# Norm sums taken four chunks at a time inside stage one, with two weight steps and a row centring moved to other places

## The chip, the cores and the metric

The kernel runs on one core of one Trainium2 chip. The metric is the device time of one execution in microseconds, the median of several runs. A core has five engines with a queue of instructions each: PE (TensorE, matrix products and transposes), DVE (VectorE), ACT (ScalarE), POOL (GpSimd) and SP (SyncE, which here only issues DMAs). Semaphores order the queues against each other; within a queue instructions start in order. A wait at the head of a queue holds all that stands behind it.

## The reference

Inputs are x and ctx, each 128 x 64 x 128 in fp32. Two layers are computed, each added to x:

```
q  = layernorm(x)                                 # no gain, no bias
pq = prob(q); pk = prob(ctx)                      # t = tanh(.)*0.499+0.5;  p = t / (sum(t) + 1e-8)
sid = (pq - pk) @ (log pq - log pk).T             # per batch, 64 x 64
att = softmax(-sid / sqrt(128)) @ ctx
f   = (ctx - att) @ W_diff.T + b_diff + q
h   = layernorm(f) * ln_g + ln_b
o   = gelu(h @ W1.T + b1) @ W2.T + b2 + f         # hidden size 512
x   = x + layernorm(o) * ln_g + ln_b
x   = x + (fp16(fp8(layernorm(x))) @ fp16(fp8(Wf)).T + bf)
```

What matters here is `prob`. With s the sum of tanh over the 128 features of a row, its norm is 0.499 s + 64. The kernel never divides: it forms pq - pk from tanh with a gain and a shift for each row, and takes log pq - log pk as the difference of two logarithms plus the logarithm of the ratio of the two norms. So for each row it needs the reciprocals of two norms, two gains, a shift and the ratio.

## The kernel before, in words

**Tiles.** The 8192 rows are 64 tiles of 128 rows (two batches each); four tiles are a chunk, so there are 16 chunks (`NC`). TQK holds the tanh of all of q and ctx, F holds q and later f and the output, X holds x plus the bias row, PV the values. The orders below are written out by hand: `run_steps` calls a function once per step, and `at(lag)` is the chunk that is `lag` steps behind. Nothing else plans the work.

**Stage one** (`phase1` on each engine) runs over the chunks. ACT takes the tanh of a ctx chunk (L507) with the sum of each row, copies two products out of PSUM (L512, L518), and takes the tanh of the q chunk two steps behind (L523). DVE takes the statistics of the x chunk (L754, then six small instructions, L711 to L726), adds the product of W_diff and its bias to F for the chunk three steps behind (L759), and makes q of the chunk one step behind (L780). POOL takes the power -0.5 of the variance (L362) and adds the bias row b to X (L368). PE transposes ctx (L951) and multiplies with W_diff (L960, L969). SP loads ctx and x; the load of x for a chunk waits for the variance of the chunk two before (L308), since the small buffers alternate, and each queue of loads is in order.

Into some steps the preparation of the weights is laid: W1 and W2 are transposed on PE at step lag 2 of chunk 6 (`W_AT`, L971), copied by DVE (L762, L764), and split in an upper and a lower part, W1h by ACT (L529), W1l by DVE in the last step before q of chunk 15 (L768). PE computes W1 times ln_b (`b1_ps`, L984) after all of stage one, and DVE adds b1 to it (L787).

**The norms** are taken by DVE in `take_norms` (L728): one instruction for 0.499 s + 64 (L735), the reciprocal (L738), then HALFK, GAINK, GAINQ, NRATIO and SHIFT (L740 to L745), small instructions over one number per row and tile. It is called for chunks 0 to 13 (`NORMS`) when chunk 13 has reached L759, and for the last two after stage one. Between its steps DVE waits for its own previous instruction.

**Stage two** runs over 17 pieces (`pairs`): 15 of four tiles and two of two. For a piece, ACT and POOL form the gain and shift of ctx in `diff_c` (L559, L380; ACT the first half of the tiles), DVE adds the part of q for three tiles (L810) and POOL for the fourth (L388, L391). ACT takes the logarithms of both sides (L569); DVE and POOL form the difference (L818; L396, L399) with LRATIO, the logarithm of NRATIO (L573). PE transposes both (L1056, L1062), ACT copies them out (L594, L596), PE forms the scores (L1044), ACT takes the exponential (L579), PE the attention product (L1029), DVE normalises it and adds it to F (L832, L838). The lags are 0, 1 and 2. Before it, DVE centres the row b2 (L678 to L682), and ACT loads another table (L533). DVE's `dve.wait_ge(pq_ready, NC)`, PE's `pe.wait_ge(pq_ready, NC)`, and POOL's and ACT's waits for `norms` stand ahead of their first pieces.

**Stage three** (`phase3`) runs over 17 pieces: the MLP, the second normalisation, the fp8 layer and the stores. The change touches nothing in it.

## Time and profile before

| | us |
|---|---|
| median of 3 runs (261.57, 262.82, 263.22) | 262.82 |
| the profiled execution | 262.99 |
| its span, as the profile has it | 261.1 |

| stage | from, to |
|---|---|
| one (tanh, products) | 0 to about 62.8 |
| change of stage | 61.5 to 66.5 |
| two (attention) | 66.5 to 128.5 |
| three | the rest |

Busy shares of the span: PE 80%, DVE 86%, ACT 83%, POOL 72%. A busy share is an average over stages; the start times of instructions show who waits. Durations of neighbouring instructions on an engine overlap a little: the start of the next one, not the end of this one, tells how fast an engine goes. TensorE runs at one of two levels of clock, and a granted clock of 0.50 is the lower one.

### The profile page before, as it was taken

Reading aid. Unit: us, or ns where it says so; the run is one execution under the profiler, and the core shown is the slowest. Engines: PE = TensorE matmul, PEld = TensorE weight load, DVE = VectorE, ACT = ScalarE, POOL = GpSimd, SP = SyncE. Lnnn points to the kernel's source line nnn. Section 1 sums busy time; section 2 is a strip of 40 time slices with the busy share of each in tenths; the row PEclk is TensorE's granted clock in tenths of the full one; section 3 lists DMA queues with packets and bytes.
Section 4 is the critical chain, followed back from the end, with each engine's and each line's share of the span. In section 5 each row is a group of like instructions: output and inputs, shape, how many; then the busy total and the mean of one; then the engine's idle time right before and its main releaser. Section 6 shows DMA issues by size and latency. Waiting matters only on the chain.

```text
span 261.1 us, 5925 instructions
## 1 busy us (share of the span) xinstructions
PE 209.4 (80%) x1723; PEld 176.3 (68%) x1723; DVE 225.0 (86%) x843; ACT 216.2 (83%) x774; POOL 188.9 (72%) x250
## 2 busy tenths in 40 slices
PE   2676676754499888887899999999999999996711
PEld 1664554533387666666689988888889888895600
DVE  2899999988879999999525889999999999999892
ACT  4599999998889999989997888988898887776521
POOL 2477666764899999991885796969697888666552
PEclk9999999795569999999999999999999999999765
DMA  5667554540000000000328189897978888977922
GB/s 140 188 201 204 158 154 135 154 113 1 1 0 3 0 3 3 1 3 4 40 32 91 12 100 135 122 133 110 151 115 132 129 125 128 137 121 121 103 61 61
DMA packets 51360, 23.65 MB, mean 91 GB/s; under 512 B 9856, under 2 KB 51200, under 8 KB 51328
## 3 DMA queue, kind: packets, MB, share of 16 engines
q0 software_dynamic: 15856, 7.87, 28.0%
q1 hardware_dynamic: 35040, 15.21, 21.9%
q10 hardware_dynamic: 432, 0.20, 0.4%
q8 instruction: 14, 0.23, 0.4%
q14 instruction: 18, 0.15, 0.2%
HBM read 9.37 MB, written 4.19 MB: 52 GB/s over the span
## 4 chain that ended last, share of the span: by engine, by line
POOL 28%; DVE 23%; ACT 20%; issue 13%; PE 11%; DMA 3%; SPq 0%; POOLq 0%; DVEq 0%; ACTq 0%
POOL F L407 7%; POOL xrstd L448 7%; ACT TQK L523 6%; ACT TQK L507 6%; POOL orstd L442 6%; DVE q_c L810 5%; POOL F L454 5%; DVE LN_c L818 5%; DVE F L838 5%; PE bank L1011 3%; ACT PV L518 3%; DMA LN_c<-in_ctx_dram 3%; ACT vT_c L512 2%; PE bank L960 1%; DVE F L863 1%
## 5 line engine op out<-in xcount | busy, mean ns | idle before, releaser
L1011 PE MATMUL bank<-W2T,TQK 128*128 128x128 f32 x512 | 68.7, 282 | 2.6 <-ACT TQK L545 2.5
L1011 PEld LDWEIGHTS bank<-W2T,TQK 128*128 128x128 f32 x512 | 64.0, 194 | 8.5 <-ACT TQK L545 4.0
L545 ACT ACTIVATE TQK<-bank,b1c 128x512 f32<-128x512 f32 (+1 forms) x68 | 44.5, 661 | 10.7 <-PE bank L1004 10.4
L448 POOL TENSOR_TENSOR xrstd<-xvar,pow_c 128x4 f32<-128x4 f32 (+1 forms) x17 | 18.5, 1090 | 23.2 <-DVE xvar L726 23.2
L362 POOL TENSOR_TENSOR xrstd<-xvar,pow_c 128x4 f32<-128x4 f32 x16 | 16.8, 1051 | 21.5 <-DVE xvar L726 21.5
L1002 PE MATMUL bank<-hTh,W1h 128*128 128x512 f32 (+1 forms) x68 | 30.4, 447 | 0.8 <-DVE hTl L801 0.8
L407 POOL DMA_DIRECT2D F<-rows x17 | 26.0, 1529 | 5.6 <-DVE E_c L796 5.6
L1003 PE MATMUL bank<-hTl,W1h 128*128 128x512 f32 (+1 forms) x68 | 26.1, 384 | 0.0
L1004 PE MATMUL bank<-hTh,W1l 128*128 128x512 f32 (+1 forms) x68 | 25.9, 382 | 0.0
L960 PE MATMUL bank<-WdT,vT_c 128*128 128x128 f32 x128 | 20.5, 309 | 4.8 <-ACT vT_c L512 4.6
L951 PE MATMUL bank<-ident,LN_c 128*128 128x128 f32 x64 | 12.3, 322 | 13.9 <-DMA LN_c<-in_ctx_dram 13.9
L960 PEld LDWEIGHTS bank<-WdT,vT_c 128*128 128x128 f32 x128 | 17.8, 215 | 7.5 <-ACT vT_c L512 7.4
L883 DVE TENSOR_SCALAR LN_c<-F,xmv,xrstd 128x128 fp8e4<-128x128 f32 x64 | 17.9, 343 | 4.8 <-POOL xrstd L448 4.6
L368 POOL TENSOR_TENSOR X<-X,rows 128x512 f32<-128x512 f32 x16 | 20.3, 1271 | 2.0 <-DVE F L780 2.0
L507 ACT ACTIVATE TQK<-LN_c 128x128 f32<-128x128 f32 x64 | 19.3, 329 | 2.3 <-DMA LN_c<-in_ctx_dram 2.3
L454 POOL DMA_DIRECT2D F<-rows x14 | 18.6, 1326 | 2.9 <-issue 2.9
L951 PEld LDWEIGHTS bank<-ident,LN_c 128*128 128x128 f32 x64 | 8.3, 162 | 18.2 <-DMA LN_c<-in_ctx_dram 18.0
L523 ACT ACTIVATE TQK<-F 128x128 f32<-128x128 f32 x64 | 19.5, 340 | 0.8 <-DVE F L780 0.8
L1029 PE MATMUL bank<-PV,E_c 64*64 64x129 f32 x256 | 18.7, 286 | 1.6 <-ACT E_c L579 1.6
L810 DVE SCALAR_TENSOR_TENSOR q_c<-TQK,GAINQ,q_c 128x128 f32<-128x128 f32 x49 | 17.8, 413 | 2.0 <-POOL q_c L380 2.0
L630 ACT ACTIVATE TQK<-F 128x128 f32<-128x128 f32 x64 | 19.0, 313 | 0.2 <-DVE F L858 0.2
L863 DVE SCALAR_TENSOR_TENSOR F<-F,orstd,rows 128x128 f32<-128x128 f32 x64 | 19.1, 359 | 0.0
(129 smaller groups left out, 645.2 us busy)
## 6 DMA issues: line engine op xcount, KB each, us to landing
F<-rows POOLq DMA_DIRECT2D x29, 256.0 KB, 4.7
LN_c<-in_ctx_dram SPq DMA_DIRECT2D x16, 256.0 KB, 3.0
X<-in_x_dram SPq DMA_DIRECT2D x16, 256.0 KB, 3.3
out_dram<-F SPq DMA_DIRECT2D x15, 256.0 KB, 2.3
LN_c<-in_L_xattn_W_dram SPq DMA_DIRECT2D x1, 256.0 KB, 3.5
lT_c<-in_L_xattn_W_dram SPq DMA_DIRECT2D x1, 256.0 KB, 3.7
F<-rows POOLq DMA_DIRECT2D x2, 128.0 KB, 4.8
out_dram<-F SPq DMA_DIRECT2D x2, 128.0 KB, 1.8
```

The lines of the kernel that those rows point to most:

```text
L407: pool.dma_start(tiles(chunk(F, k)), over_tiles(b2_r, k.g), accum_op=ALU.add).then_inc(b2_added[k.n % 3], 16)
L448: pool.tensor_tensor(buf(xrstd, x1, G), buf(xvar, x1, G), pow_c[:, 0:x1.g], ALU.pow).then_inc(x1_rstd, 1)
L454: pool.dma_start(tiles(chunk(F, x1)), over_tiles(bf_r, x1.g), accum_op=ALU.add).then_inc(bf_added[x1.n % 3], 16)
L507: last = act.activation(all_tile(TK, k, i), tile(ctx_c, k, i), ACT.Tanh, accum_out=per_tile(SUMK, k, i))
L523: last = act.activation(all_tile(TQ, k, i), all_tile(F, k, i), ACT.Tanh, accum_out=per_tile(SUMQ, k, i))
L545: act.activation(hid(m, j), m1_bank(m, j), ACT.Gelu, bias=b1c[:, j:j + 1]).then_inc(gelu_ready, 1)
L810: last = dve.scalar_tensor_tensor(out=tile(diff_c, k, i), in0=all_tile(TQ, k, i), scalar=per_tile(GAINQ, k, i), in1=tile(diff_c, k, i), op ...
L960: last = pe.matmul(P_B[k.n % 3][:, i * D:(i + 1) * D], tile(vT_c, k, i), WdT[:, :], start=(i == 0), stop=False, skip_group_check=True)
L1002: pe.matmul(ps, w_hi, buf(hTh, m), start=True, stop=False)
L1003: pe.matmul(ps, w_hi, buf(hTl, m), start=False, stop=False)
L1004: pe.matmul(ps, w_lo, buf(hTh, m), start=False, stop=True).then_inc(m1_ps, 1)
L1011: last = pe.matmul(M2_B[m.buf][:, i * D:(i + 1) * D], hid(m, j)[:, i * D:(i + 1) * D], W2T[:, j * D:(j + 1) * D], start=(j == 0 and i == 0 ...
```

## The change

1. `take_norms` is cut in three: `norm_sums`, `norm_inverses`, `norm_gains`. They are called for four chunks at a time (`NORM_CUTS`), the first three groups inside stage one, when chunks 4, 8 and 12 reach L759, with the statistics laid between sum and reciprocal and q between reciprocal and gains. The last group is taken in stage two behind piece 1.
2. W1l moves from the last step to the step in which chunk 10 reaches L759; the products for b1 on PE and DVE's addition of b1 move to the steps of chunks 10 and 11.
3. The centring of the b2 row moves from ahead of stage two to behind piece 2.
4. POOL forms all four tiles of `diff_c` for piece 0, those of piece 1 right behind its part of piece 0, and adds the bias row to X of chunk 15 only behind piece 15 of stage two. ACT has no tile of piece 0. POOL's scratch tile is another.
5. LRATIO is taken in two calls: chunks 0 to 11 ahead of the first logarithms, the rest behind those of piece 10.
6. Waits: each engine waits for the group of norms that a piece needs (`wait_norms`) when the piece begins a group. PE enters stage two when 14 chunks, not 16, have reached L759, and waits for the rest and for b1 ahead of the first attention product.

```diff
@@ -89,7 +89,8 @@
     EARLY = 2
-    NORMS = NC - 2
+    NORM_CUTS = (0, 4, 8, 12, NC)
+    LRATIOS = NORM_CUTS[-2]
@@ -174,7 +175,7 @@
         r16_c = LN_c[:, 2 * C:3 * C].bitcast(F16)
-        qpart_c = RNORM[:, :]
+        qpart_c = E_c[:, C:C + D]
@@ -196,7 +197,11 @@
         def by_act(k):
-            return k.g // 2
+            return k.g // 2 if k.n > 0 else 0
+        def wait_norms(eng, k):
+            if k.live and k.n in NORM_CUTS[:-1]:
+                eng.wait_ge(norms, NORM_CUTS.index(k.n) + 1)
@@ -271,7 +276,8 @@
         vT_ps, vT_sb, P_ps, P_sb = sem("vT_ps"), sem("vT_sb"), sem("P_ps"), sem("P_sb")
-        norm_step, halfk_ready, norms, lratio = sem("norm_step"), sem("halfk_ready"), sem("norms"), sem("lratio")
+        norm_sum, norm_inv, halfk_ready, norms, lratio = (
+            sem("norm_sum"), sem("norm_inv"), sem("halfk_ready"), sem("norms"), sem("lratio"))
@@ -354,6 +360,11 @@
             pool.memset(PV[:, :].rearrange("p (t w) -> p t w", w=D + 1)[:, :, D:D + 1], -1.0).then_inc(consts, 1)
+            def add_to_x(k):
+                pool.wait_ge(q_ready, k.n + 1)
+                pool.tensor_tensor(tiles(chunk(X, k)), tiles(chunk(X, k)), over_tiles(b_r, k.g),
+                                   ALU.add).then_inc(xb_ready, 1)
@@ -361,45 +372,50 @@
                 k = at(1)
-                if k.live:
-                    pool.wait_ge(q_ready, k.n + 1)
+                if k.live and k.n < NC - 1:
...
                         pool.wait_ge(br_in, 16)
-                    pool.tensor_tensor(tiles(chunk(X, k)), tiles(chunk(X, k)), over_tiles(b_r, k.g),
-                                       ALU.add).then_inc(xb_ready, 1)
+                    add_to_x(k)
             run_steps(chunks, 1, phase1)
+            def kparts(k):
+                wait(pool, dT_ps, k.n - 1)
+                wait_norms(pool, k)
+                for i in range(by_act(k), k.g):
+                    last = pool.tensor_scalar(tile(diff_c, k, i), all_tile(TK, k, i), per_tile(GAINK, k, i),
+                                              per_tile(SHIFT, k, i), ALU.mult, ALU.add)
+                last.then_inc(kpart, 1)
...
                 if k.live:
-                    wait(pool, dT_ps, k.n - 1)
-                    if is_piece(k, NORMS):
-                        pool.wait_ge(norms, 2)
-                    for i in range(by_act(k), k.g):
-                        last = pool.tensor_scalar(tile(diff_c, k, i), all_tile(TK, k, i), per_tile(GAINK, k, i),
-                                                  per_tile(SHIFT, k, i), ALU.mult, ALU.add)
-                    last.then_inc(kpart, 1)
+                    if k.n > 1:
+                        kparts(k)
...
                         pool.wait_ge(kpart, k.n + 1)
-                        if is_piece(k, 0):
-                            pool.wait_ge(norms, 2)
...
                                            ALU.add).then_inc(diff_pool, 1)
+                        if is_piece(k, 0):
+                            kparts(pairs[1])
...
                             pool.wait_ge(lratio, 1)
+                        if is_piece(k, LRATIOS):
+                            pool.wait_ge(lratio, 2)
...
                                            ALU.subtract).then_inc(lr_pool, 1)
-            pool.wait_ge(norms, 1)
+                if is_piece(k, NA - 2):
+                    add_to_x(chunks[NC - 1])
+            kparts(pairs[0])
@@ -553,8 +569,7 @@
                 wait(act, dT_ps, k.n - 1)
-                if is_piece(k, NORMS):
-                    act.wait_ge(norms, 2)
+                wait_norms(act, k)
@@ -568,9 +583,9 @@
                                    scale=TANH_GAIN).then_inc(ln_ready, 1)
-                if is_piece(k, 0):
-                    act.wait_ge(norms, 2)
-                    act.activation(LRATIO[:, :], NRATIO[:, :], ACT.Ln).then_inc(lratio, 1)
+                if is_piece(k, LRATIOS - 2):
+                    act.wait_ge(norms, len(NORM_CUTS) - 1)
+                    act.activation(LRATIO[:, LRATIOS * G:], NRATIO[:, LRATIOS * G:], ACT.Ln).then_inc(lratio, 1)
@@ -613,8 +628,8 @@
             act.wait_ge(sel_ready, 1)
-            act.wait_ge(norms, 1)
-            kparts(pairs[0])
+            act.wait_ge(norms, len(NORM_CUTS) - 2)
+            act.activation(LRATIO[:, 0:LRATIOS * G], NRATIO[:, 0:LRATIOS * G], ACT.Ln).then_inc(lratio, 1)
@@ -725,18 +740,25 @@
                 dve.tensor_tensor(buf(xvar, k, G), buf(xgap, k, G), mv[:, :, 1], ALU.add).then_inc(done, 1)
-            def take_norms(first, end, part):
-                cols, n = slice(first * G, end * G), 2 * part
-                sums, norm, rnorm = (t[:, :].rearrange("p (s t) -> p s t", s=2)[:, :, cols] for t in (SUM, NORM, RNORM))
-                dve.wait_ge(tanh_k, end)
-                dve.wait_ge(tanh_q, end)
+            def of_norms(part):
+                cols = slice(NORM_CUTS[part] * G, NORM_CUTS[part + 1] * G)
+                return cols, [t[:, :].rearrange("p (s t) -> p s t", s=2)[:, :, cols] for t in (SUM, NORM, RNORM)]
+            def norm_sums(part):
+                cols, (sums, norm, rnorm) = of_norms(part)
+                dve.wait_ge(tanh_k, NORM_CUTS[part + 1])
+                dve.wait_ge(tanh_q, NORM_CUTS[part + 1])
                 dve.tensor_scalar(norm, sums, TANH_GAIN, TANH_SHIFT * D + PROB_EPS,
-                                  ALU.mult, ALU.add).then_inc(norm_step, 1)
-                dve.wait_ge(norm_step, n + 1)
-                dve.reciprocal(rnorm, norm).then_inc(norm_step, 1)
-                dve.wait_ge(norm_step, n + 2)
+                                  ALU.mult, ALU.add).then_inc(norm_sum, 1)
+            def norm_inverses(part):
+                cols, (sums, norm, rnorm) = of_norms(part)
+                dve.wait_ge(norm_sum, part + 1)
+                dve.reciprocal(rnorm, norm).then_inc(norm_inv, 1)
+            def norm_gains(part):
+                cols, (sums, norm, rnorm) = of_norms(part)
+                dve.wait_ge(norm_inv, part + 1)
@@ -744,7 +766,9 @@
                                          op0=ALU.mult, op1=ALU.subtract).then_inc(norms, 1)
-                dve.wait_ge(norms, part + 1)
+            def norm_part(r):
+                return NORM_CUTS.index(r.n) - 1 if r.live and r.n in NORM_CUTS[1:] else None
@@ -762,17 +786,24 @@
                     dve.tensor_copy(W2T[:, :], bank[4][:, :]).then_inc(wt_sb, 1)
-                if is_piece(q, NC - 1):
+                if is_piece(r, W_AT + 4):
...
                                              op1=ALU.subtract).then_inc(w_done, 1)
+                if is_piece(r, W_AT + 5):
+                    dve.wait_ge(b1_ps, 1)
+                    dve.tensor_tensor(b1c[:, :], bank[5][:, 0:HB], b1_raw[:, :], ALU.add).then_inc(b1_ready, 1)
+                part = norm_part(r)
+                if part is not None:
+                    norm_sums(part)
...
                     stats_var(s, x_terms, x_var)
+                if part is not None:
+                    norm_inverses(part)
@@ -780,15 +811,10 @@
                     last.then_inc(q_ready, 1)
-                if is_piece(r, NORMS - 1):
-                    take_norms(0, NORMS, 0)
-                    dve.wait_ge(b1_ps, 1)
-                    dve.tensor_tensor(b1c[:, :], bank[5][:, 0:HB], b1_raw[:, :], ALU.add).then_inc(b1_ready, 1)
+                if part is not None:
+                    norm_gains(part)
             run_steps(chunks, 3, phase1)
-            take_norms(NORMS, NC, 1)
@@ -804,8 +830,9 @@
                 if k.live:
-                    dve.wait_ge(kpart_act, k.n + 1)
+                    wait(dve, kpart_act, k.n)
                     dve.wait_ge(kpart, k.n + 1)
+                    wait_norms(dve, k)
@@ -814,11 +841,20 @@
                         dve.wait_ge(lratio, 1)
+                    if is_piece(k, LRATIOS):
+                        dve.wait_ge(lratio, 2)
...
                     last.then_inc(lr_ready, 1)
+                if is_piece(k, 1):
+                    norm_sums(len(NORM_CUTS) - 2)
+                    norm_inverses(len(NORM_CUTS) - 2)
+                    norm_gains(len(NORM_CUTS) - 2)
+                if is_piece(k, 2):
+                    dve.wait_ge(rows_in, 16 * 3)
+                    centre_row(b2_r, 2).then_inc(rows_ready, 1)
@@ -847,8 +883,6 @@
                     lower_half(pieces[1])
-            dve.wait_ge(rows_in, 16 * 3)
-            centre_row(b2_r, 2).then_inc(rows_ready, 1)
@@ -975,14 +1009,14 @@
                     last.then_inc(w_ps, 1)
+                if is_piece(k, W_AT + 4):
+                    pe.wait_ge(w1u_sb, 1)
+                    for j in range(HB):
+                        last = pe.matmul(bank[5][:, j:j + 1], W1u[:, j * D:(j + 1) * D], b_col[:, :],
+                                         start=True, stop=True)
+                    last.then_inc(b1_ps, 1)
             run_steps(chunks, 2, phase1)
-            pe.wait_ge(wt_sb, 1)
-            for j in range(HB):
-                last = pe.matmul(bank[5][:, j:j + 1], W1u[:, j * D:(j + 1) * D], b_col[:, :], start=True, stop=True)
-            last.then_inc(b1_ps, 1)
@@ -1018,6 +1052,9 @@
                     turn_h(pieces[0])
+                if is_piece(k, 0):
+                    pe.wait_ge(b1_ready, 1)
+                    pe.wait_ge(pq_ready, NC)
@@ -1062,7 +1099,7 @@
                     last.then_inc(lT_ps, 1)
-            pe.wait_ge(pq_ready, NC)
+            pe.wait_ge(pq_ready, NC - 2)
...
             run_steps(pairs, 2, phase2)

```

## Rows read from the trace of the kernel before

**Rows 1.** the page, busy time of each engine (share of the span, instructions)

```profile
PE 209.4 (80%) x1723; PEld 176.3 (68%) x1723; DVE 225.0 (86%) x843; ACT 216.2 (83%) x774; POOL 188.9 (72%) x250
```

**Rows 2.** the chain that ended last, stage one (start, us, what)

```profile
52.64 1.17 ACT TQK L507 x8
...
55.93 1.17 ACT TQK L507 x8
```

**Rows 3.** timeline of DVE, end of stage one and change (start, us, instruction, [idle before])

```profile
41.16 1.11 DVE L780 TENSOR_SCALAR F<-X,xmv,xrstd 128x128 f32<-128x128 f32 x4
42.18 0.86 DVE L754 BATCH_NORM_STATS2 xstat<-X 128x6 f32<-128x128 f32 x4
42.96 0.67 DVE L759 TENSOR_TENSOR F<-bank,F 128x512 f32<-128x512 f32 x1
...
44.25 1.11 DVE L780 TENSOR_SCALAR F<-X,xmv,xrstd 128x128 f32<-128x128 f32 x4
...
59.26 0.69 DVE L759 TENSOR_TENSOR F<-bank,F 128x512 f32<-128x512 f32 x1 [0.88 <-ACT TQK L523]
59.87 0.74 DVE L768 SCALAR_TENSOR_TENSOR W1l<-bank,g_col,W1h 128x512 fp32r<-128x512 f32 x1
60.53 1.11 DVE L780 TENSOR_SCALAR F<-X,xmv,xrstd 128x128 f32<-128x128 f32 x4
61.55 0.22 DVE L735 TENSOR_SCALAR NORM<-SUM 128x112 f32<-128x112 f32 x1
...
63.51 0.16 DVE L787 TENSOR_TENSOR b1c<-bank,b_raw 128x4 f32<-128x4 f32 x1
...
64.79 0.17 DVE L735 TENSOR_SCALAR NORM<-SUM 128x16 f32<-128x16 f32 x1
...
65.78 0.29 DVE L678 TENSOR_REDUCE row_mean<-rows 128x1 f32<-128x128 f32 x1
...
66.49 1.18 DVE L810 SCALAR_TENSOR_TENSOR q_c<-TQK,GAINQ,q_c 128x128 f32<-128x128 f32 x3
```

**Rows 4.** timeline of ACT, start of stage two

```profile
62.97 1.28 ACT L533 ACT_TABLE_LOAD   x1
64.26 0.88 ACT L559 ACTIVATE q_c<-TQK,SHIFT,GAINK 128x128 f32<-128x128 f32 x2
65.05 1.13 ACT L569 ACTIVATE LN_c<-TQK,half_c 128x1024 f32<-128x1024 f32 x1
66.09 0.24 ACT L573 ACTIVATE LRATIO<-NRATIO 128x64 f32<-128x64 f32 x1
...
69.05 0.60 ACT L594 ACTIVATE vT_c<-bank 128x512 f32<-128x512 f32 x1 [0.92 <-PE bank L1056]
```

**Rows 5.** the chain that ended last, PE at the start of stage two

```profile
70.69 1.12 PE bank L1044 x16
...
73.71 1.94 PE bank L1029 x16
```

**Rows 6.** busy time by stretch, one slice (engines, then granted clock, DMA share, GB/s)

```profile
74.00:75.00 1.00, 1.00 (x14) 1.00 (x12) 0.90 (x3) 1.00 (x3) 0.92 (x3) 0.50 0.00 0
```

**Rows 7.** timeline of DVE, stage two

```profile
76.99 1.18 DVE L810 SCALAR_TENSOR_TENSOR q_c<-TQK,GAINQ,q_c 128x128 f32<-128x128 f32 x3
...
83.91 1.12 DVE L810 SCALAR_TENSOR_TENSOR q_c<-TQK,GAINQ,q_c 128x128 f32<-128x128 f32 x3
...
118.30 0.61 DVE L810 SCALAR_TENSOR_TENSOR q_c<-TQK,GAINQ,q_c 128x128 f32<-128x128 f32 x2
```

**Rows 8.** the loads of x, all 16

```profile
DMA to landing us min/median/max: 2.8/3.3/7.0
```

**Rows 9.** timeline of POOL, end of stage one, first and last pieces of stage two

```profile
58.46 1.27 POOL L368 TENSOR_TENSOR X<-X,rows 128x512 f32<-128x512 f32 x1
...
63.59 0.89 POOL L380 TENSOR_SCALAR q_c<-TQK,GAINK,SHIFT 128x128 f32<-128x128 f32 x2 [0.60 <-DVE SHIFT L745]
...
116.35 1.04 POOL L380 TENSOR_SCALAR q_c<-TQK,GAINK,SHIFT 128x128 f32<-128x128 f32 x2
```

## The prediction

> **What bounds the kernel now.** I read the busy shares first, then the chain that ended last, then each engine's rows around the change of stage. No engine is busy over the whole span; DVE with 86% and ACT with 83% lead [rows 1], so each stage is read by itself.
>
> Stage one goes by ACT. The chain runs along ACT from one group of tanh to the next, 3.29 us per chunk [rows 2]. DVE is close behind: its q instructions of chunks 10 and 11 start 3.09 us apart in two steps in which it waits for nothing [rows 3], so it has 0.20 us to spare in each step. After two steps with an extra weight copy it is behind ACT by 0.8 us at 42.96; at the end it waits 0.88 us for ACT [rows 3].
>
> At the change of stage DVE is the chain. W1l, q of chunk 15, the norms of 14 chunks (61.55 to 63.51), b1, two additions, the norms of the last two (64.79 to 65.78) and the centring of the b2 row (65.78 to 66.49) stand in a line before the first gain instruction of stage two [rows 3]. ACT has loaded its table at 62.97, begins its first logarithm at 65.05 and is not what the others wait for [rows 4].
>
> The start of stage two goes by PE: from the first scores at 70.69 to the end of the first attention product, 73.71 + 1.94 = 75.65, PE works at the low clock without a break [rows 5]; the granted clock is 0.50, the 1.2 GHz level, in the slice just before the end of it [rows 6]. DVE begins piece 3 at 76.99 [rows 7]. From there it waits for nothing: the ten steps from piece 5 at 83.91 to piece 15 at 118.30 are 3.44 us each [rows 7]. So each microsecond by which piece 3 comes earlier is one off the end of stage two. Stage three comes behind it with nothing of the change in it, and I let it shift whole.
>
> **The change, part by part.** All against the profiled execution: span 261.1, time 262.99, so 1.9 around the span; it stands 0.17 above the median, 262.82.
>
> Norms inside stage one. The two calls of before cost 1.96 us for 14 chunks and 0.99 for two [rows 3]; on a line through both, four chunks alone are 1.15. Laid between other instructions, the steps no longer wait out each other's ends. Bounds 0.4 (no more than the last five small instructions) and 1.15; I take 0.8, because three of the gaps go. Three such parts lie in stage one.
>
> W1l and b1 move into stage one as well: 0.66 (59.87 to 60.53) and 0.1 of the 0.16 of the row at 63.51, the rest overlapping [rows 3]. Now the bookkeeping for DVE, which has 0.20 spare per step. Part 0 comes two steps before the weight copies, so 0.8 less 2 x 0.2, that is 0.4, is left and carried to 42.96, giving 43.36. From there to the addition of chunk 13 are five steps, 5 x 3.09 = 15.45; two parts, 1.6; W1l and b1, 0.76; less 0.86 for the first statistics (the row at 42.18), which the last step has no chunk for. The sum is 60.3. The addition starts at 60.3 and not at 59.26: the cover is gone and DVE paces the end of stage one. It then does q at once (W1l is not between any more): 60.9 against 60.53. So q of chunk 15 is ready **0.4 late**. With parts at 0.4 it would be 0.7 early (then ACT bounds it, 59.26 + 0.61 = 59.87); with parts at 1.15, 1.3 late.
>
> The loads of x wait for the variances, so they are issued later too, but DVE's own need for them is later by as much; the need comes two steps, 6.2, after the statistics of the chunk whose variance frees the buffer, and that variance 2.4 into its step; 3.8 us are left, and landing takes 3.3 (median), 2.8 at best, 7.0 at worst [rows 8]. I price that at nothing; its cover is 0.5 us. On SP the row loads stand behind the last x load; they are wanted at 73.
>
> b1's matmuls on PE lie in stage one now, where PE waits for loads; nothing.
>
> After q. ACT's last four tanh take 1.17 [rows 2], so the addition of chunk 15 is 62.1 + 1.2 + 0.6 = 63.95 (rounded up to 64.1 for the waits) and the first gain instruction follows **at 64.1 instead of 66.49**.
>
> GpSimd. It used to end stage one with the addition to X of chunk 14 at 58.46 (1.27), then 15, and its part of chunk 0 took 0.89 for two tiles [rows 9]. Now the addition of 14 comes after q of 14, about 60.0 to 61.3, then four tiles, 1.8, ready at 63.1: before DVE's 64.1, with 1.0 to spare. The addition of 15 goes behind piece 15 of stage two. What queues behind it is the last piece's tile; GpSimd has the last two ready by 117.4 (116.35 + 1.04) [rows 9], and DVE wants the last one only after the whole of piece 15, which it begins at 118.30 [rows 7]: at least two pairs, 1.2, and an attention product's 1.3 later. 1.27 lies inside 3.4. Nothing.
>
> ACT. The table load shifts with the tanh: 63.4 + 1.28. Its two tiles of chunk 0 (0.79, 64.26 to 65.05) are gone, the first LRATIO call (0.15 of a row of 0.24, the rest overlapping) stands before the logarithm: it runs from 64.8 instead of 65.05 and ends at 65.9. DVE, done with its gains at 65.2, **waits here 0.7 us, a new wait**. Behind it on ACT: tiles of chunk 1, 0.79; logarithm 1, 1.04; two copies, 0.49 each (0.60 less the overlap) [rows 4]. That is 65.9 + 2.81 = 68.7, and the first scores start at 68.75 instead of 70.69, 1.9 earlier. PE then has its 4.96 us at the low clock: 73.7 instead of 75.65.
>
> DVE meanwhile: logarithm differences 0 to 67.05, piece 1 (2.13) to 69.2, the last norms (1.05, alone) to 70.25, piece 2 to 72.4, centring (0.71) to 73.1. It still waits 0.6 for PE. So the last norms and the centring, which I cost at nothing, lie under PE; without that cover they are 1.76. Sum: **1.9 us off**, 261.1 from 262.99. Against the median it would be 260.9; I give 261.0.
>
> Unknown is when the clock rises. PE is busy without a break from 68.75 where it was from 70.69. If it rises before the first attention product, DVE bounds at 73.1, piece 3 begins at 74.4, and 2.5 are gained. If it rises one step later than PE's own shift, that step costs PE about 5.0 against DVE's 3.44 [rows 5, 7], 1.5 lost.
>
> **DVE beside GpSimd.** In stage two, three gain instructions take 1.12 beside GpSimd's work; when GpSimd is through, two take 0.61 [rows 7]. Less 0.08 for the end of the last, that is 0.35 and 0.26 each. So GpSimd slows one by 0.09, not by a whole instruction of its own (0.89 for two, 0.44) [rows 9]. The Trainium skill (SBUF — State Buffer, section "SBUF: two separate sides") says that the port pair that both share is an exclusive lock held for the whole instruction. By that rule GpSimd's tiles, which begin at 61.3 while DVE is at q of chunk 15 (60.9 to 61.95), would hold the two instructions left of it by 0.44 each, and the sum would be 1.0 off instead of 1.9. The rows show a partial cost, 2 x 0.09 here, and I leave it out of the sum.
>
> **The rivals.**
> - *Forecast*, 0.52: gain 0.8 to 2.6, likeliest 1.9, that is 260.2 to 262.0 by the median. For it: PE's unbroken 4.96 us. Against it: its last 0.6 hangs on the clock.
> - *DVE's line is the whole cost*, 0.22: norm parts at 0.5 or less, or the clock up early; gain 2.6 to 3.3. The bound is what DVE's line loses, 66.49 to 63.4, 3.1. Time 259.5 to 260.2. For it: the spaces between small instructions are 0.08. Against: PE's low clock.
> - *Another pace of stage two, quicker*, 0.08: GpSimd comes into it with a lead over DVE of 1.4 instead of 0.8 us, and the instructions that collide are others. A tenth less on 3.44 over 12 steps is 1.2 more: 259.7, at best 258.5.
> - *The same, slower*, 0.10: the place is DVE's six two-operand instructions per step, which bear 6 x 0.09 = 0.5 of contention. If half as much comes on top (0.26), 12 steps cost 3.1 and the time is 262.82 - 1.9 + 3.1 = 264.0; twice as much, 267. It decides against the change from 0.16 a step on. Against it: the pace has been steady at 3.44 for 12 steps, as if the two had settled.
> - *q of chunk 15 is held*, 0.08: two of its instructions wait out one of GpSimd's each, 2 x 0.44 = 0.9, or the norm parts cost their 1.15, which makes q 1.3 late and not 0.4. Either leaves 1.0 of gain, 261.8; both together, 262.7. For it: the two do slow each other in stage two. Against it: only by 0.09. The lock of the page named above is this case.
>
> **The numbers.** 261.0 is the forecast's likeliest. The range of 8 in 10, 258.8 to 263.2, takes in the early clock with a quicker pace below, and the held q above; out stay the slow pace and half of the extremes. What can be told from no change is 1%, 2.6 us: faster than 260.2 is the second and third case, 0.30; slower than 265.4 is the far half of the slow pace and accidents that I don't see, 0.07; the rest 0.63.
>
> **What would show it.** In the profile after: DVE's addition of chunk 13 near 60.3 with no wait before it; its first gain instruction near 64.1, then an idle of 0.7 released by ACT's logarithm; first scores near 68.75; a DVE wait of 0.6 for the attention product; piece 3 at 75.1; steps of 3.44 after it. Wrong would be: a DVE wait for ACT of over 0.3 before the addition of chunk 13 (the parts are cheap), an idle before the statistics released by a load of x, a step other than 3.44 in stage two, or a stage three whose length from the last piece on is not that of before.

## The result: no gain, a little slower, and the profile after

The changed kernel takes 263.89 us (median of 7 runs, 263.49 to 264.10) against 263.07 for the kernel before on the same chip (7 runs, 261.57 to 263.22). The ratio is 1.0041, with a 95% interval of 1.0023 to 1.0059. Forecast were 1.9 us less. The profiled execution took 263.58 us with a span of 261.7, that is 0.6 more than before in both.

The busy shares, to be set beside [rows 1]:

```profile
PE 208.4 (80%) x1723; PEld 175.8 (67%) x1723; DVE 228.0 (87%) x857; ACT 215.6 (82%) x773; POOL 190.7 (73%) x252
```

DVE has 14 instructions more and 3.0 us more busy time. The small instructions of a norm group start 0.08 us apart and a reciprocal takes 0.35, so fourteen of them should add some 1.5 us: something in them is longer than it should be. The timeline of DVE around the change of stage answers to [rows 3] and, from 77.33 on, to [rows 7] (start, us, instruction, idle before it):

```profile
31.49 1.27 DVE L765 TENSOR_TENSOR NRATIO<-NORM,RNORM 128x16 f32<-128x16 f32 x1
...
44.00 0.67 DVE L783 TENSOR_TENSOR F<-bank,F 128x512 f32<-128x512 f32 x1
...
61.47 0.17 DVE L763 TENSOR_SCALAR GAINK<-RNORM 128x16 f32<-128x16 f32 x1
61.54 0.16 DVE L764 TENSOR_SCALAR GAINQ<-RNORM 128x16 f32<-128x16 f32 x1
61.62 1.25 DVE L765 TENSOR_TENSOR NRATIO<-NORM,RNORM 128x16 f32<-128x16 f32 x1
62.80 0.16 DVE L767 SCALAR_TENSOR_TENSOR SHIFT<-RNORM,HALFK 128x16 f32<-128x16 f32 x1
62.88 0.68 DVE L783 TENSOR_TENSOR F<-bank,F 128x512 f32<-128x512 f32 x1
63.49 1.10 DVE L811 TENSOR_SCALAR F<-X,xmv,xrstd 128x128 f32<-128x128 f32 x4
...
66.65 0.88 DVE L837 SCALAR_TENSOR_TENSOR q_c<-TQK,GAINQ,q_c 128x128 f32<-128x128 f32 x3
68.52 0.99 DVE L847 SCALAR_TENSOR_TENSOR LN_c<-LN_c,LRATIO 128x128 f32<-128x128 f32 x3 [0.99 <-ACT LN_c L584]
...
76.01 0.24 DVE L868 RECIPROCAL nrden<-bank 128x2 f32<-128x2 f32 x2
...
77.33 1.18 DVE L837 SCALAR_TENSOR_TENSOR q_c<-TQK,GAINQ,q_c 128x128 f32<-128x128 f32 x3
...
115.44 1.18 DVE L837 SCALAR_TENSOR_TENSOR q_c<-TQK,GAINQ,q_c 128x128 f32<-128x128 f32 x3
118.90 0.60 DVE L837 SCALAR_TENSOR_TENSOR q_c<-TQK,GAINQ,q_c 128x128 f32<-128x128 f32 x2
```

NRATIO, 16 numbers per partition, takes 1.25 us; its neighbours of the same size take 0.16. The reader is to see that DVE does not wait by the profile: there is no idle behind these rows, the time is inside the instruction. The line of the source has all four of them (duration in ns, least, median, greatest):

```profile
L765 DVE TENSOR_TENSOR NRATIO<-NORM,RNORM x4: 168/1258/1266, 31.5 to 72.7; 128x16 f32<-128x16 f32 x4
```

Three of four, the three in stage one, are long. What runs beside them is in the timeline of GpSimd (it answers to [rows 9]):

```profile
31.44 1.28 POOL L365 TENSOR_TENSOR X<-X,rows 128x512 f32<-128x512 f32 x1 [0.16 <-DVE F L811]
...
61.57 1.27 POOL L365 TENSOR_TENSOR X<-X,rows 128x512 f32<-128x512 f32 x1 [0.16 <-DVE F L811]
62.84 1.91 POOL L386 TENSOR_SCALAR q_c<-TQK,GAINK,SHIFT 128x128 f32<-128x128 f32 x4
...
68.59 0.77 POOL L410 TENSOR_SCALAR LN_c<-LN_c,LRATIO 128x128 f32<-128x128 f32 x1 [1.74 <-ACT LN_c L584]
```

The addition to X waits for q, and the gains stand right behind q on DVE. So GpSimd starts its 1.27 us at 61.57, DVE starts NRATIO 0.05 later, and NRATIO ends as the addition does (61.62 + 1.25 = 62.87, against 61.57 + 1.27 = 62.84). The same at 31.44 and 31.49. The order of the change makes them meet each time. I call such an instruction held: it is in progress, by the profile, until the one on GpSimd ends.

ACT and PE at the start of stage two, beside [rows 4] and [rows 5]:

```profile
65.92 1.28 ACT L549 ACT_TABLE_LOAD   x1
67.21 0.24 ACT L632 ACTIVATE LRATIO<-NRATIO 128x48 f32<-128x48 f32 x1
67.36 1.13 ACT L584 ACTIVATE LN_c<-TQK,half_c 128x1024 f32<-128x1024 f32 x1
```

```profile
70.05 1.09 PE L1099 MATMUL bank<-ident,LN_c 128*128 128x128 f32 x4 [1.17 <-POOL LN_c L413]
71.91 1.12 PE L1081 MATMUL bank<-vT_c,lT_c 128*64 128x64 f32 x16 [0.78 <-ACT lT_c L611]
...
74.86 1.10 PE L1066 MATMUL bank<-PV,E_c 64*64 64x129 f32 x16
```

The first scores are 1.2 later than before, not 1.9 earlier. The clock gives part of it back. The stretches (engines' busy time, then granted clock, DMA share, GB/s), beside [rows 6]:

```profile
74.00:75.00 1.00, 1.00 (x7) 0.67 (x7) 1.00 (x4) 0.63 (x2) 0.94 (x2) 0.59 0.00 0
75.00:76.00 1.00, 1.00 (x18) 0.83 (x18) 0.93 (x5) 1.00 (x3) 0.92 (x3) 1.00 0.00 0
```

The granted clock goes from 0.50 to 1.00, from the 1.2 to the 2.4 GHz level, within 74 to 75, and the attention product takes 1.10 instead of 1.94. From the first scores to its end are 4.05 us instead of 4.96. DVE's reciprocal at 76.01 no longer waits for it. So piece 3 starts at 77.33, only 0.34 later than before. The twelve steps to 118.90 are 3.465 us each instead of 3.44, another 0.26, and stage three has its old length. 0.34 + 0.26 = 0.60 is the difference of the spans.

### The profile page after: what moved, and what is told of

Its sections match the earlier page's. It is cut to its first block, busy times and chain, and to the rows that moved or that the text cites. A ratio compares the mean times of both kernels' runs of the same rounds, so it can differ in the third digit from the quotient of the medians.

```text
span 261.7 us, 5946 instructions
## 1 busy us (share of the span) xinstructions
PE 208.4 (80%) x1723; PEld 175.8 (67%) x1723; DVE 228.0 (87%) x857; ACT 215.6 (82%) x773; POOL 190.7 (73%) x252
## 4 chain that ended last, share of the span: by engine, by line
POOL 42%; DVE 20%; issue 16%; ACT 10%; PE 8%; DMA 3%; SPq 0%; POOLq 0%; DVEq 0%; ACTq 0%
POOL F L423 7%; POOL xrstd L464 7%; POOL orstd L458 6%; POOL F L470 5%; POOL q_c L386 4%; DVE F L811 4%; POOL LN_c L410 3%; PE bank L1045 3%; POOL E_c L398 3%; ACT TQK L539 3%; DMA LN_c<-in_ctx_dram 3%; DVE xstat L778 2%; POOL q_c L401 2%; POOL LN_c L413 2%; ACT TQK L523 2%
## 5 line engine op out<-in xcount | busy, mean ns | idle before, releaser
L1045 PE MATMUL bank<-W2T,TQK 128*128 128x128 f32 x512 | 67.9, 279 | 2.6 <-ACT TQK L561 2.5
L1045 PEld LDWEIGHTS bank<-W2T,TQK 128*128 128x128 f32 x512 | 63.0, 191 | 8.8 <-ACT TQK L561 4.2
L994 PE MATMUL bank<-WdT,vT_c 128*128 128x128 f32 x128 | 21.8, 324 | 8.2 <-DVE F L783 7.3
L994 PEld LDWEIGHTS bank<-WdT,vT_c 128*128 128x128 f32 x128 | 19.5, 233 | 11.0 <-issue 5.9
L539 ACT ACTIVATE TQK<-F 128x128 f32<-128x128 f32 x64 | 19.2, 323 | 1.9 <-DVE F L811 1.8
L1066 PE MATMUL bank<-PV,E_c 64*64 64x129 f32 x256 | 17.9, 276 | 1.9 <-ACT E_c L594 1.7
L847 DVE SCALAR_TENSOR_TENSOR LN_c<-LN_c,LRATIO 128x128 f32<-128x128 f32 x49 | 18.3, 425 | 1.0 <-ACT LN_c L584 1.0
L645 ACT ACTIVATE TQK<-F 128x128 f32<-128x128 f32 x64 | 19.0, 314 | 0.2 <-DVE F L892 0.2
L566 ACT ACTIVATE TQK<-F 128x128 f32<-128x128 f32 x64 | 18.8, 299 | 0.0
```

The source lines that it names most:

```text
L539: last = act.activation(all_tile(TQ, k, i), all_tile(F, k, i), ACT.Tanh, accum_out=per_tile(SUMQ, k, i))
L994: last = pe.matmul(P_B[k.n % 3][:, i * D:(i + 1) * D], tile(vT_c, k, i), WdT[:, :], start=(i == 0), stop=False, skip_group_check=True)
L1045: last = pe.matmul(M2_B[m.buf][:, i * D:(i + 1) * D], hid(m, j)[:, i * D:(i + 1) * D], W2T[:, j * D:(j + 1) * D], start=(j == 0 and i == 0 ...
```

## The experiments

Twelve kernels, each timed in several rounds against the kernel before on the same chip. "Ratio" is to that kernel; the chip is not the same for all twelve, so they are compared with each other by their ratios. The diffs are against the kernel named.

**e1: the gains one step later.** Against the changed kernel: `norm_gains` is called one step after `norm_inverses`, ahead of the statistics, when GpSimd's addition is over.

```diff
+                part, late = norm_part(r), gains_part(r)
...
+                if late is not None and s.live:
+                    norm_gains(late)
...
-                if part is not None:
-                    norm_gains(part)
+                if late is not None and not s.live:
+                    norm_gains(late)
```

> The changed kernel, with one thing moved: the five gain instructions of a group of norms (HALFK to SHIFT) come one step later, ahead of the statistics (for the third group behind q of chunk 15), when GpSimd is past its addition to X. Theory one, the held instruction: NRATIO, which reads two SBUF tensors, took 1.26 us three times because it waits out GpSimd's 1.27 us addition that started just before it; here it takes 0.2, DVE's line is 3 x 1.1 = 3.3 us shorter, q of chunk 15 ends near 61.5 instead of 64.5, the first scores start near 69 instead of 71.9, and the time is 261.2 (260.3 to 262.0), below the kernel before. Theory two, too much laid into stage one: three groups, W1l and b1 are more than DVE's spare time carries, wherever they stand; q of chunk 15 still ends after 63.3 and the time is 263.3 or more.

Measured: 260.64 us, ratio 0.9930 (0.9905 to 0.9954). NRATIO by its line, then DVE and GpSimd around q of chunk 15:

```profile
L765 DVE TENSOR_TENSOR NRATIO<-NORM,RNORM x4: 167/168/172, 32.8 to 69.6; 128x16 f32<-128x16 f32 x4
```

```profile
59.21 0.68 DVE L786 TENSOR_TENSOR F<-bank,F 128x512 f32<-128x512 f32 x1
59.81 1.71 DVE L816 TENSOR_SCALAR F<-X,xmv,xrstd 128x128 f32<-128x128 f32 x4
...
63.59 0.92 DVE L842 SCALAR_TENSOR_TENSOR q_c<-TQK,GAINQ,q_c 128x128 f32<-128x128 f32 x3
...
73.71 0.24 DVE L873 RECIPROCAL nrden<-bank 128x2 f32<-128x2 f32 x2 [0.78 <-PE bank L1071]
...
75.03 1.07 DVE L842 SCALAR_TENSOR_TENSOR q_c<-TQK,GAINQ,q_c 128x128 f32<-128x128 f32 x3
```

```profile
59.39 1.28 POOL L365 TENSOR_TENSOR X<-X,rows 128x512 f32<-128x512 f32 x1 [0.16 <-DVE F L816]
```

NRATIO is 0.168 in all four places, with no instruction added or removed. DVE is busy for 225.0 us with its 857 instructions, 3.0 less than in the changed kernel. Against the ratio of the change, 1.0041, the gain is 1.1% or 2.9 us. The rest of the change is therefore worth 0.7% against the kernel before, and the place of five small instructions costs more than that. Now q of chunk 15 is what meets the addition: four take 1.71 instead of 1.11. The third group of gains runs beside GpSimd's gain tiles, and its NRATIO is not held there:

```profile
61.77 0.17 DVE L765 TENSOR_TENSOR NRATIO<-NORM,RNORM 128x16 f32<-128x16 f32 x1
```

```profile
60.66 1.88 POOL L386 TENSOR_SCALAR q_c<-TQK,GAINK,SHIFT 128x128 f32<-128x128 f32 x4
```

**e2: the held instruction behind a short one.** Against the changed kernel: GpSimd's addition to X for chunks 6, 10 and 14, which run beside the gains, is four instructions of one tile.

```diff
+                if k.n in (6, 10, 14):
+                    for i in range(k.g):
+                        last = pool.tensor_tensor(all_tile(X, k, i), all_tile(X, k, i), b_r, ALU.add)
+                    last.then_inc(xb_ready, 1)
+                    return
```

> The changed kernel with DVE's queue untouched; GpSimd's addition to X of chunks 6, 10 and 14 is done as four instructions of one tile instead of one of four. Theory one: DVE waits only for the instruction of GpSimd that is in progress, so NRATIO takes at most 0.6 us in place of 1.26, 3 x 0.7 = 2 us come off DVE's line and the time is 262.0 (261.3 to 262.8), though GpSimd itself works some 0.5 us longer in each of the three steps. Theory two: no change, 263.9. A third theory, bandwidth shared while both run: NRATIO is as long as before or longer, since GpSimd now works longer beside it, 263.9 or more.

Measured: 261.93 us, ratio 0.9975 (0.9959 to 0.9991).

```profile
L770 DVE TENSOR_TENSOR NRATIO<-NORM,RNORM x4: 166/450/458, 31.4 to 70.4; 128x16 f32<-128x16 f32 x4
```

```profile
59.92 1.77 POOL L367 TENSOR_TENSOR X<-X,rows 128x128 f32<-128x128 f32 x4
```

NRATIO falls from 1.26 to 0.45, about one of the four short instructions (1.77 / 4 = 0.44). The length of the hold follows the length of GpSimd's instruction, and nothing on DVE was touched. GpSimd pays 0.5 for the cutting, and 0.28 of each hold is left; 0.45% lies between this kernel and e1, and their intervals just miss each other.

**e5 and e6: which instructions are held.** Against the kernel before: behind the first statistics instruction of chunks 3 to 7, beside GpSimd's addition, DVE gets one instruction of 8 columns whose result nobody reads, in e5 with two inputs in SBUF, in e6 with one.

```diff
+                            dve.tensor_tensor(scr[:, s.n * 8:s.n * 8 + 8], pow_c[:, :], eps_c[:, :], ALU.mult)
```

```diff
+                            dve.tensor_scalar(scr[:, s.n * 8:s.n * 8 + 8], pow_c[:, :], 2.0, None, ALU.mult)
```

> The kernel before the change, with one small extra instruction on DVE in the steps of chunks 3 to 7: a tensor_tensor over 8 columns that reads two constant SBUF tiles, placed behind the first of the four statistics instructions, while GpSimd is in its 1.27 us addition to X. Nothing uses what it writes. Held-instruction theory: each takes 0.9 to 1.2 us instead of 0.16, some 5 us in DVE's line against 0.2 spare per step, so DVE paces these steps and the kernel is 2 to 4 us slower. Rival, that NRATIO was long by its own kind or place in the change: 0.16 each, no change in time.

> The same as the run with the two-input instruction, but the extra instruction is a tensor_scalar over 8 columns that reads one constant SBUF tile. If only instructions with two SBUF inputs are held: 0.16 us each, five of them hidden in DVE's spare time, no change. If a plain fp32 tensor_scalar from SBUF to SBUF is held as well, as the first q instruction of chunk 15 in e1 suggests (0.94 us, ending when GpSimd's addition ended), it is as slow as the run with two inputs, 2 to 4 us more.

Measured: e5 266.11 us, ratio 1.0137 (1.0100 to 1.0175); e6 265.96 us, ratio 1.0133 (1.0095 to 1.0171). The added line in each, e5 first:

```profile
L759 DVE TENSOR_TENSOR scr<-pow_c,eps_c x5: 1253/1255/1269, 15.1 to 32.2; 128x8 f32<-128x8 f32 x5
```

```profile
L759 DVE TENSOR_SCALAR scr<-pow_c x5: 1260/1264/1273, 14.9 to 32.0; 128x8 f32<-128x8 f32 x5
```

Both forms are held through the whole addition: five instructions of 8 columns cost the kernel 3.5 to 3.6 us. What is not held beside the same additions are the statistics (four in 0.86 to 0.87, there as elsewhere) and DVE's additions with an input in PSUM (0.67 to 0.69 with and without GpSimd beside them). That is why stage one of the kernel before hardly shows it: beside GpSimd stand just such instructions.

**e3: W1l back at its old place.** Against e1.

```diff
-                if is_piece(r, W_AT + 4):
+                if is_piece(q, NC - 1):
```

> The kernel of e1 with W1l alone put back to where it stood before the change, ahead of q of chunk 15. Theory one: DVE has 0.66 less in its line earlier and the same 0.66 more just before q of chunk 15; it is worth 0 to 0.4 us, 261.2 to 261.6. Theory two: the move of W1l is part of the overload, so putting it back makes the end of stage one earlier and the kernel 0.5 us or more faster than e1.

Measured: 260.75 us, ratio 0.9931 (0.9904 to 0.9959), no difference from e1. W1l is 0.74 at 59.89 here; q of chunk 15 comes after it at 60.55 and takes 1.11, unheld. In e1 q starts at 59.81 and is held for 0.6. Both end within 0.15 of each other: what the move of W1l saves, the hold takes.

**e4 and e9: chunk 0 shared by ACT and GpSimd as before.** e4 against e1: `by_act` as before, `kparts(pairs[0])` on ACT, GpSimd's tiles of piece 1 in their old place, the addition of chunk 15 in stage one. e9 against e4: the third group of gains behind the addition to F of chunk 15, and ACT's tiles ahead of its wait for the norms' third group. The diff is that of e4.

```diff
-            return k.g // 2 if k.n > 0 else 0
+            return k.g // 2
...
-                if k.live and k.n < NC - 1:
+                if k.live:
...
-                        if is_piece(k, 0):
-                            kparts(pairs[1])
```

> The kernel of e1 with chunk 0 of stage two shared by ACT and GpSimd as before the change, LRATIO behind the first logarithm and the addition to X of chunk 15 in stage one. Theory one: the first logarithm stands behind 0.79 us of tiles on ACT instead of 0.15 of LRATIO, and DVE waits for it, so 0.6 us slower than e1, 261.8. If the chip's clock or another path bounds the start of stage two, the same as e1.

> As e4 (gains one step later, chunk 0 shared by ScalarE and GpSimd, chunk 15's addition to X inside stage one), but the third group of gains stands behind the addition of chunk 15, where no addition of GpSimd runs beside it, and ScalarE does not wait for the last norms before its tiles of chunk 0. Theory (e4 lost its 1.8 us against e1 mostly to the hold of that third group, 1.1 us, and to ScalarE's wait): this kernel gives about 261.3 us, 0.6 to 0.8 behind e1 (260.64). Rival (sharing chunk 0 between the engines costs the 1.8 us by itself, in whatever order): 262.5 as e4, with the third group at 0.17 us and the first gain instruction still at 65.6 or the tiles still ready late.

Measured: e4 262.51 us, ratio 0.9999 (0.9983 to 1.0016); e9 262.59 us, ratio 0.9992 (0.9978 to 1.0006). In e4 the third NRATIO is held again (1.25 at 62.17, beside the addition of chunk 15), so I took 1.1 of the 1.9 us for that. e9 takes the hold away and stays where e4 is: that reading was wrong, and the rival of e9 stands. The rows of e4 say why: its first gain instruction, at 65.62, has waited 0.92 for ACT's tiles, so the hold before it was covered. DVE in e9:

```profile
64.62 0.16 DVE L760 TENSOR_TENSOR NRATIO<-NORM,RNORM 128x16 f32<-128x16 f32 x1
...
65.91 0.88 DVE L835 SCALAR_TENSOR_TENSOR q_c<-TQK,GAINQ,q_c 128x128 f32<-128x128 f32 x3 [1.04 <-issue]
...
69.78 1.07 DVE L835 SCALAR_TENSOR_TENSOR q_c<-TQK,GAINQ,q_c 128x128 f32<-128x128 f32 x3 [1.71 <-POOL q_c L386]
```

DVE waits 1.04 at 65.91, where ACT's two tiles of chunk 0 run from 64.94 behind the table load, and 1.71 at 69.78 for GpSimd's tiles of piece 1, which stand again behind its wait for the logarithm. So the fourth part of the change, which I had counted with only 0.8 for ACT's two tiles, carries nearly all of what e1 gains: by the medians of one chip, e1 is 2.0 us under the kernel before and e4 0.1. How it splits between the first tiles, piece 1 and the place of the addition was not tried. The profiled executions differ by more, and not by this part alone: e4's addition at 29.15 is already 0.5 behind e1's at 28.64, where both have the same instructions, and e9 waits 0.54 for a load of x at 32.04, which e1 does not.

**e7: GpSimd idle during q of chunk 15.** Against e1: the additions to X of chunks 14 and 15 both stand behind the last pieces of stage two, and GpSimd waits for q of chunk 15.

```diff
-                if k.live and k.n < NC - 1:
+                if k.live and k.n < NC - 2:
...
+                    add_to_x(chunks[NC - 2])
+                if is_piece(k, NA - 1):
                     add_to_x(chunks[NC - 1])
+            pool.wait_ge(q_ready, NC)
             kparts(pairs[0])
```

> The kernel of e1, with GpSimd kept idle while DVE makes q of chunk 15: the addition to X of chunk 14 goes behind piece 15 of stage two and that of chunk 15 behind piece 16, and GpSimd waits for q of chunk 15 before its tiles of chunk 0. In e1 the four q instructions took 1.63 us in place of 1.02, beside GpSimd's addition. Held-instruction theory: q takes 1.02, all of the start of stage two comes 0.6 earlier, and GpSimd's tiles are still ready before DVE wants them; 0.3 to 0.6 us faster than e1, 260.2. If TensorE's low clock bounds the start of stage two at a fixed place, no change against e1.

Measured: 260.17 us, ratio 0.9913 (0.9882 to 0.9944). DVE:

```profile
60.42 1.11 DVE L819 TENSOR_SCALAR F<-X,xmv,xrstd 128x128 f32<-128x128 f32 x4
...
63.85 1.08 DVE L845 SCALAR_TENSOR_TENSOR q_c<-TQK,GAINQ,q_c 128x128 f32<-128x128 f32 x3
```

q takes 1.11 without the addition beside it and 1.71 with it. In this execution q itself starts 0.6 later than in e1 (DVE waited 0.33 for a load of x at 31.84), so nothing reaches the first gain instruction, and the intervals of e1 and e7 overlap: the hold of q is shown, a gain from removing it is not.

**e8: the last norms and the centring ahead of stage two.** Against e1.

```diff
-                if is_piece(k, 1):
-                    norm_sums(len(NORM_CUTS) - 2)
...
-                if is_piece(k, 2):
-                    dve.wait_ge(rows_in, 16 * 3)
-                    centre_row(b2_r, 2).then_inc(rows_ready, 1)
...
+            norm_sums(len(NORM_CUTS) - 2)
...
+            centre_row(b2_r, 2).then_inc(rows_ready, 1)
```

> The kernel of e1, with the last group of norms and the centring of the b2 row put back ahead of stage two, as before the change. In e1 DVE waits 0.95 us for the first logarithm and 0.78 us for the first attention product. If the first gain instruction is 1.8 us later, the first wait takes up about 0.95 of it; 0.9 us slower than e1, 261.5. If all of it is hidden under the logarithm and TensorE, no change; if nothing is, 1.8 slower.

Measured: 261.26 us, ratio 0.9954 (0.9933 to 0.9975). The first gain instruction starts 1.8 later than in e1 (65.39 against 63.59), but DVE then waits 2.20 for the attention product at 74.40 where it waited 0.78, and piece 3 is 0.7 later (75.71 against 75.03). So of 1.8 us put on the path 0.7 arrive: PE and ACT bound most of this stretch, as forecast, but not all.

**e10, e11 and e12: the order of GpSimd's instructions in stage two.** From piece 2 on, GpSimd's part of q stands ahead of its gain tiles. e10 is e7 with it, e11 the kernel before with nothing else, e12 is e1 with it.

```diff
+                    if k.n > 1 and k.g == G:
+                        wait_norms(pool, k)
+                        wait(pool, diff_pool, k.n)
+                        pool.tensor_scalar(qpart_c, all_tile(TQ, k, G - 1), per_tile(GAINQ, k, G - 1), None,
+                                           ALU.mult).then_inc(qpart, 1)
                     if k.n > 1:
                         kparts(k)
```

> As e7 (GpSimd idle during q of chunk 15), with GpSimd's part of q ahead of its gain tiles in every step from piece 2 on, so that other instructions of VectorE and GpSimd meet. Theory (the step of stage two is 3.465 us instead of 3.438 because of which of the two engines' instructions meet, not because of GpSimd's total work): the step moves from 3.465, to 3.44 or less where fewer meet (0.3 us or more over twelve steps, about 259.9), or up where VectorE then waits for GpSimd's gain tiles. Rival (GpSimd's total work sets the step): 3.465 as in e7, and 260.2 us.

> The kernel before, with one edit: GpSimd's part of q stands ahead of its gain tiles in every step of stage two from piece 2 on. Theory (the order of GpSimd's instructions sets which of them meet VectorE's, and so the step): the step goes from 3.44 to 3.32 us, 12 x 0.12 = 1.4 us less, about 261.3 us. Rival (the 3.32 us of e10 hangs on the early lead that GpSimd gets there): the step stays at 3.44 and the time at 262.7 us.

> As e1 (the changed kernel with the gains one step later), with the same order of GpSimd's instructions in stage two. Both parts add if the theories hold: stage one as in e1 (third group of gains not held, first gain instruction at 63.6), step 3.32 instead of 3.465 us, 12 x 0.145 = 1.7 us less, minus 0.9 if GpSimd's late addition to X still holds one of VectorE's last logarithm differences: 259.0 to 259.9 us. Rival (what stage two gains is given back in stage three): 260.6 as e1.

Measured: e10 259.98 us, ratio 0.9903 (0.9878 to 0.9929); e11 262.05 us, 0.9974 (0.9964 to 0.9983); e12 260.17 us, 0.9903 (0.9889 to 0.9917). One step of e10, and its last but two, which is longer; then GpSimd there:

```profile
97.39 1.19 DVE L851 SCALAR_TENSOR_TENSOR q_c<-TQK,GAINQ,q_c 128x128 f32<-128x128 f32 x3
98.50 0.99 DVE L861 SCALAR_TENSOR_TENSOR LN_c<-LN_c,LRATIO 128x128 f32<-128x128 f32 x3
...
100.71 1.19 DVE L851 SCALAR_TENSOR_TENSOR q_c<-TQK,GAINQ,q_c 128x128 f32<-128x128 f32 x3
...
111.76 1.92 DVE L861 SCALAR_TENSOR_TENSOR LN_c<-LN_c,LRATIO 128x128 f32<-128x128 f32 x3
```

```profile
112.24 1.29 POOL L365 TENSOR_TENSOR X<-X,rows 128x512 f32<-128x512 f32 x1
```

e10 and e12 have the lowest ratios of the study, 1.0% below the kernel before, but their intervals overlap those of e7 and e1, the kernels without the edit; only e11, against the kernel before, shows a gain by its time. The step is 3.32 in e10 (3.465 in e7); in e11 and e12 it alternates between about 3.45 and 3.30, 3.38 on average (3.44 and 3.465 without the edit). DVE and GpSimd do the same instructions on the same data in all of them; only which ones meet is different. So the step is set by the meetings, not by either engine's sum of work. The order alone doesn't decide who meets: e10 and e12 have the same order from piece 2 on and another step, and so have e5 (3.44) and e6 (3.465), which are the kernel before in stage two. e11 gains 0.8 us of the 1.4 forecast, since every second step stays long; its rival, that the 3.32 of e10 hangs on the lead with which GpSimd comes into stage two, is not excluded. e12 misses its forecast of 259.0 to 259.9 by 0.3. In e10 the deferred addition, 1.29 at 112.24, holds one logarithm difference (1.92 for three), which takes back 0.9. e10's stage two ends 1.4 earlier than e7's in the profiled executions, and the medians differ by 0.2; the profiled execution of e7 was 0.8 above its median and that of e10 0.4 below. What their other executions do in stage two no trace shows.

## Why the prediction was wrong

| step of the prediction | forecast | after | e1, without the hold |
|---|---|---|---|
| DVE's addition at 42.96 before | 43.36 | 44.00 | 42.88 |
| addition of chunk 13 | 60.3 | 62.88 | 59.21 |
| q of chunk 15 starts | 60.9 | 63.49 | 59.81 |
| first gain instruction | 64.1 | 66.65 | 63.59 |
| DVE waits for the first logarithm | 0.7 | 0.99 | 0.95 |
| first scores | 68.75 | 71.91 | 68.85 |
| DVE waits for the attention product | 0.6 | none | 0.78 |
| piece 3 | 75.1 | 77.33 | 75.03 |
| step of stage two | 3.44 | 3.465 | 3.465 |

**The step that failed** is the price of a norm group inside stage one: 0.8, with 1.15 as the upper bound. It cost about 0.65 and 1.1 of hold (1.26 less 0.16), 1.75 in all, three times. The slack of ACT took some of the first, which leaves 0.64 at 44.00; the other two bring 2 x 1.1 less 2 x 0.15 for the cheaper rest, 1.9. Their sum, 2.5, is the 2.6 by which the addition of chunk 13 is late against the forecast (62.88 - 60.3). My bounds came from two calls, and I moved those instructions without asking what runs on GpSimd at the new place. The first of the two calls even has the addition of chunk 15 beside it, but meets it with the reciprocal:

```profile
61.72 1.26 POOL L368 TENSOR_TENSOR X<-X,rows 128x512 f32<-128x512 f32 x1 [1.99 <-DVE F L780]
```

```profile
61.80 0.85 DVE L738 RECIPROCAL RNORM<-NORM 128x112 f32<-128x112 f32 x1
...
62.69 0.34 DVE L740 TENSOR_SCALAR HALFK<-RNORM 128x56 f32<-128x56 f32 x1
```

The reciprocal starts inside the addition and ends before it, at 62.65: it isn't held, and its 0.85 goes with its columns (0.25 for 16 of them and 0.34 for 32, with no addition beside them). HALFK has 0.34 instead of the 0.18 of its neighbour of the same size at 62.95 and ends at 63.03, when the addition does (62.98): 0.16 of hold was all that this call showed. The addition to X was in [rows 9] with its 1.27, and its place, right behind q, is in the code. What follows of it: piece 3 is 2.2 late against the forecast (77.33 - 75.1) and the pace of stage two adds 0.3, together the 2.5 between the span and its forecast (261.7 against 261.1 - 1.9).

**The rule was on the table and I averaged it away.** I took three gain instructions in 1.12 against 0.26 each alone as a cost of 0.09 each, a partial sharing. In the step at 83.91 of the kernel before, the instructions of a group are not equal. By their lines (duration in ns, least, median, greatest):

```profile
L810 DVE SCALAR_TENSOR_TENSOR q_c<-TQK,GAINQ,q_c x3: 337/454/485, 83.9 to 84.7; 128x128 f32<-128x128 f32 x3
```

```profile
L818 DVE SCALAR_TENSOR_TENSOR LN_c<-LN_c,LRATIO x3: 347/371/602, 85.0 to 85.8; 128x128 f32<-128x128 f32 x3
```

Of the three of L818, one takes 0.60 and another 0.35; their mean shows neither. Stage one of that kernel has the plain case, DVE first, then GpSimd:

```profile
13.07 0.36 DVE L711 TENSOR_TENSOR xmv<-xstat 128x8 f32<-128x8 f32 x1
```

```profile
12.13 1.27 POOL L368 TENSOR_TENSOR X<-X,rows 128x512 f32<-128x512 f32 x1
```

L711 takes 0.36 instead of 0.16 and ends when the addition does (13.07 + 0.36 = 13.43, against 12.13 + 1.27 = 13.40). A hold costs what is left of GpSimd's instruction. In stage two its two-input instructions are 0.46 to 0.51 us long, so little is left on average; beside an addition of 1.27 the held instruction becomes eight times as long. The Trainium skill (SBUF — State Buffer, section "SBUF: two separate sides") states just this, an exclusive lock for the whole instruction and no sharing of bandwidth, for a VectorE instruction with two SBUF inputs or in a two-port mode, a condition that the prediction left out; the three NRATIO of the change in stage one, e2, e5 and e6 agree with the lock, the NRATIO beside GpSimd's gain tiles in e1 does not.

**The rival came true in another place.** I gave "q of chunk 15 is held" 0.08 and put the hold on GpSimd's gain tiles. In the changed kernel those tiles run from 62.84 to 64.75 beside q at 63.49, and q takes 1.10, as ever. The two holds of 0.44 that the prediction worked out for that place don't show. What holds is the addition to X, and what it holds are three NRATIO; in e1 it is q, by 0.6.

**What was right.** e1 differs from the change in the place of the gains alone, and the forecast of piece 3 is met there within 0.1 (75.03 against 75.1), the time by its ratio as well: 0.7% off 262.82 is 261.0. It is partly luck, for two errors cancel in it: DVE's line is 0.5 to 1.1 earlier than forecast, and the first scores come 4.56 after the first logarithm starts instead of 3.95, since PE's second transposes wait for GpSimd's share of the logarithm difference, a step that I left out. The unbroken 4.96 of PE at the low clock nearly holds in e1 (68.85 to 71.80 + 1.86 = 73.66 are 4.81, with a granted clock of 0.50 up to 73 and 0.80 from 73 to 74) and not in the changed kernel, where the clock rises before the attention product.

**Stage two.** "Another pace, slower" had 0.10 and its price was over 0.16 a step; it is 0.025, 0.3 in all. The changed kernel, e1, e3, e4, e7 and e8 settle at 3.465, e9 at 3.45; the kernel before and e2, which has the change with other additions to X, at 3.44. Of e5 and e6, which differ from the kernel before in stage one alone, the one is at 3.44 and the other at 3.465, so it isn't the change's order in stage two that picks. What does stays open.

**Not moved.** Stage three is as long as before, the loads of x release nothing late in the changed kernel, and the deferred addition of chunk 15 (1.27 at 117.80) ends before DVE's last piece needs it. For two of these three the nothing was thin: the profiled executions of e7 and e9 wait 0.33 and 0.54 for a load right behind the first norm group, and in e10 the deferred addition holds an instruction by 0.9. In the changed kernel it stands beside DVE's instructions with an input in PSUM (1.13 at 117.86, as ever).

**Slips in the prediction's working.** The q instructions at 41.16 and 44.25 are those of chunks 9 and 10. Parts at 1.15 make q of chunk 15 1.4 late, not 1.3. The last norms are four chunks, so 1.15 by the prediction's own line and not 1.05 (they take 1.2 in the changed kernel, 71.77 to 72.95). An early clock gives 2.6, not 2.5 (76.99 - 74.4). None of them changes the account above.

## What to carry to other kernels

Before an instruction of VectorE is moved, look at what GpSimd runs at the new place: a `tensor_tensor` or `tensor_scalar` of VectorE on fp32 in SBUF can cost there the whole rest of GpSimd's instruction, however small it is itself, so small ones belong where GpSimd is idle or beside its gain tiles, where they lost 0.1 at most here. An instruction that GpSimd starts on the end of a VectorE instruction meets the very next ones, each time. And look for a hold in the duration of single instructions, against the least of the same shape, not in the mean of a group or in the idle times.

## What the runs showed of the hardware

- A VectorE instruction of 8 columns with one fp32 input in SBUF is held as long as one with two: 1.264 against 1.255 us, beside an addition of 1.26 on GpSimd. The Trainium skill names `tensor_scalar` among the operations that can take both port pairs (SBUF — State Buffer, section "Who interferes with whom"); e6 agrees.
- q's instructions, of the same form with 128 columns, were held by a two-input instruction of GpSimd of 1.28 us (1.71 for four, e1) and not visibly by its one-input tiles of 0.48 (1.10 for four, the changed kernel). Nor was a NRATIO, which has two inputs in SBUF, held beside those tiles (0.17 at 61.77, e1, and at 72.70, the changed kernel); HALFK and SHIFT there lose 0.1 each (0.27 at 61.44 and 61.86, e1). Why is open.
- It isn't the length of GpSimd's instruction alone: its power instruction of 4 columns takes 1.05 us (57.43, the kernel before), and q beside it takes its usual 1.11 (57.27).
- Not held beside the addition to X: the statistics, additions with an input in PSUM, and a reciprocal from SBUF (0.85 for 112 columns, the kernel before).
- The same instructions on both engines take 3.32, 3.38, 3.44 or 3.465 us a step, by which of them meet; their order is one thing that moves it, and e5 and e6 show that it isn't the only one.
